# One-hot compares of a graph network kernel read their index row from PSUM instead of SBUF

## The chip, the cores and the metric

The kernel runs on one core of a Trainium2 chip. The metric is the device time of one execution in microseconds, as the median of several runs.

## The reference

Two graph layers over 6250 nodes and 100000 edges, sorted by destination. First three SAGE layers, each a mean over incoming edges and two products of 128 x 128:

```python
def _sage_layer(x, src, dst, Wl_i, bl_i, Wr_i):
    msg = x[src]
    agg = jax.ops.segment_sum(msg, dst, num_segments=N_NODES)
    cnt = jax.ops.segment_sum(jnp.ones((src.shape[0],), x.dtype), dst, num_segments=N_NODES)
    mean = agg / jnp.clip(cnt, 1.0)[:, None]
    return mean @ Wl_i + bl_i + x @ Wr_i
```

Then a gated graph convolution with 16 attributes for each edge (sigmoid times softplus of a linear map of both nodes and the attributes, summed by destination, batch norm, layer norm, relu), with a residual and a layer norm after either part.

## The kernel before, in words

**Tiles and windows.** The nodes are 49 windows of 128. The edges are cut into 832 tiles (`NS`) of at most 128 edges, and each tile belongs to one window. `dlo` holds, in column t, the row of the window to which each of the 128 edges of tile t goes; `srcs` holds the edges' source nodes; both stay in SBUF. `iota` is a tile of 128 x 128 in SBUF with 0 to 127 in each row.

**A SAGE layer** has two parts. The second, after the sums, makes the new features window by window (L999 to L1014 on VectorE, transposes and products on TensorE, copies on ScalarE) and writes the product to `y_dram`. The first sums the gathered rows and is a loop of 52 turns with 16 tiles each (`UB`), on four engines at once. For one tile:

- GpSimd (L421) gathers 128 rows of 512 bytes from `y_dram` to slot u of `msg` with an indirect DMA. Its indices come from `idx`.
- ScalarE (L677) copies eight columns of `srcs` to one half of `idx`, as soon as TensorE has summed the eight tiles that used that half's message slots one turn earlier (it waits for `tiles_summed`).
- VectorE makes the one-hot matrix of the tile (L963): `iota` is compared with one column of `dlo`, a scalar for each partition, and gives 128 x 128 fp32 in one of four slots of `oh4`.
- TensorE (L511) multiplies the one-hot matrix by the message slot into PSUM bank u mod 4. It waits for the gather, for the one-hot and for that bank's last add. An fp32 product shows as a pair of matmuls.
- VectorE (L974) adds the bank's 128 x 129 to the tile's window of `acc` (a dynamic offset); each add waits for the add before it.

VectorE's order in a turn is written out: load the 16 window offsets from `regs` (L946), one-hots 0, 1 and 2, add 0, one-hot 3, add 1, and so on, so that a one-hot stands two tiles ahead of its add. Before each of them stand register operations that compute the semaphore value to wait for or the offset (L971, L972, and those of L963 and L974); they run on VectorE's sequencer. Layer 3's turns 0 to 45 also split edge attributes in bf16 parts (L662, L667, L953) which SyncE writes back (L320).

**The convolution** (its one-hots and adds run from 4288 to 5672 us) gathers in the same manner (L439), four tiles a step. Its one-hots are made four tiles at a time by a tensor-tensor compare (L1156), its adds are L1127, its register operations L1125 among others.

**PSUM** is eight banks of 512 fp32. The sums use banks 0 to 3. `ps_tr` is banks 4 to 7 cut in 16 slots of 128; the transposes of the row numbers at the start use slots 0 to 6 and 8 to 14 (L500), those of the layers slots 0 to 6. The convolution uses all banks.

Of the kernel before, what the change touches and what calls it, by code (L numbers as in the profile page):

```python
# [5 lines left out]
P = 128  # L6
# [9 lines left out]
UB = 16  # L16
# [17 lines left out]
def build_gnn(nc, x, xT, src, dst, ea, eaT, w0, bl, blT, w1, we, b1, bn, out):  # L34
# [11 lines left out]
    with ctx:  # L46
        def sb(name, shape, dt=f32):
            return ctx.enter_context(nc.sbuf_tensor(name, shape, dt))
# [29 lines left out]
        dlo = sb("dlo", [P, NC * P])  # L78
# [4 lines left out]
        iota = sb("iota", [P, P])  # L83
        ident = sb("ident", [P, P])
# [26 lines left out]
        oh4 = work[:, 3584:4096].rearrange("p (u f) -> p u f", f=P)  # L111
# [72 lines left out]
        ps = ctx.enter_context(nc.psum_tensor("ps", [P, 8, 512], f32))  # L184
# [5 lines left out]
        ps_pre = ps[:, 0:4, :].rearrange("p (g b) (h f) -> p g (b h) f", g=2, h=2)  # L190
        ps_ohT = ps[:, 4:6, :].rearrange("p g (t f) -> p g t f", t=G)
        ps_agg = ps[:, 6:8, :].rearrange("p g (t f) -> p g t f", t=G)

        names = """const loads dnat w0_in xT_first xT_rest y_written products dve cnt S
            tki tab tab_back idx_given idx_sorted ea_sorted rows rowsf rows_tr dlo_ready srcs_ready
# [41 lines left out]
        def _(sp):  # L237
# [67 lines left out]
            for k, (_, part_) in enumerate(EA_GROUPS):  # L305
                sp.dma_start(we_rows[k * ED:(k + 1) * ED, :], we_part[:, part_, :]).then_inc(s["we_in"], 16)
# [8 lines left out]
            def store_parts(n):  # L315
                for part_, ready in enumerate(("ea_1", "ea_2", "ea_3")):
                    sp.wait_ge(s[ready], n + 1)
                    for k, (mine, _) in enumerate(EA_GROUPS):
                        if mine == part_:
                            sp.dma_start(parts_flat[k, :, bass.ds(n * EA_C, EA_C)], ea_part[part_])\  # L320
                                .then_inc(s["ea_written"], 16)
                sp.wait_ge(s["ea_written"], (n + 1) * (16 * len(EA_GROUPS)))
                sp.sem_inc(s["ea_free"], 1)
# [140 lines left out]
        def _(pe):  # L464
            te = nc.tensor
# [4 lines left out]
            for it in range(NCH):  # L470
# [3 lines left out]
                for b, wins in enumerate(PAIRS):  # L474
                    for u in wins:
                        w = it * CW + u
                        last = te.matmul(ps_prod[:, u, :], lhsT=xT_sb[:, w * P:(w + 1) * P], rhs=w0_sb[:, 0, :],
                                         start=True, stop=True)
# [16 lines left out]
                        .then_inc(s["f_rank"], 1)  # L495

            pe.wait_ge(s["rowsf"], 1)
            for c in range(2 * NC):
                rows, slot = (d_rowsf, c) if c < NC else (s_rowsf, c - NC + 8)
                last = te.transpose(ps_tr[:, slot, :], rows[:, c % NC * P:(c % NC + 1) * P], ident[:, :])  # L500
# [41 lines left out]
            with pe.Fori(0, NCH) as it:  # L542
# [6 lines left out]
                for b, wins in enumerate(PAIRS):  # L549
# [3 lines left out]
                    for h in range(2):  # L553
                        for u in wins:
                            last = te.matmul(ps[:, 2 + b % 2 if h else P_BANKS[b], u % 2 * 2 * F:(u % 2 + 1) * 2 * F],  # L555
                                             lhsT=hT[:, u, :],
                                             rhs=w1_sb[:, h * 2 * F:(h + 1) * 2 * F], start=True, stop=True)
# [58 lines left out]
            for w in range(0, NW, 4):  # L616
                n = min(4, NW - w)
                last = te.matmul(ps[:, 0, 0:n * F], lhsT=ones[:, :], rhs=a3[:, w:w + n, 0:F],
                                 start=w == 0, stop=w + n == NW)
            last.then_inc(s["bn_sum"], 1)  # L620
            for i, w in enumerate(range(0, NW, 4)):
# [3 lines left out]
                          rhs=work[:, 5376 + i % 2 * 512:5376 + i % 2 * 512 + n * F],  # L625
                          start=w == 0, stop=w + n == NW).then_inc(s["sq_used"], 1)
# [205 lines left out]
        def _(dve):  # L832
            v = nc.vector
# [111 lines left out]
            def load_windows(first):  # L945
                dve.reg_load(w_regs, regs[0:1, bass.ds(first, UB)])  # L946
                return [dve.snap(r, min_val=0, max_val=(NW - 1) * FA) for r in w_regs]  # L947

            def ea_rest(n, k):

                dve.wait_ge(s[f"ea_{k}"], n + 1)
                alone(dve)
                v.tensor_tensor(ea_chunk(n), ea_chunk(n), ea_part[k - 1], ALU.subtract).then_inc(s[f"ea_r{k}"], 1)  # L953

            def sage_adds(layer, a=0, b=NS // UB, split=False):
                with dve.Fori(a, b) as it:
                    wins = load_windows(it * UB)
                    first = layer * NS + it * UB

                    def onehot(u):  # L960

                        dve.wait_ge(s["tiles_summed"], first + u + 13)
                        v.tensor_scalar(oh4[:, u % 4, :], iota[:, :], dlo[:, bass.ds(it * UB + u, 1)], None,  # L963
                                        ALU.is_equal).then_inc(s["onehots"], 1)

                    onehot(0)
                    onehot(1)
                    for u in range(UB):
                        if u + 2 < UB:
                            onehot(u + 2)  # L970
                        dve.wait_ge(s["tiles_summed"], first + u + 17)  # L971
                        dve.wait_ge(s["tiles_added"], first + u + 4)  # L972
                        a = acc[:, bass.ds(wins[u], FA)]
                        v.tensor_tensor(a, a, ps[:, u % 4, 0:FA], ALU.add).then_inc(s["tiles_added"], 1)  # L974
                        if split and u % (UB // 2) == UB // 2 - 1:
                            ea_rest(it, u // (UB // 2) + 1)
# [288 lines left out]
```

## Time and profile before

| What | Value |
|---|---|
| Median of 3 runs | 5962.75 us (5954.95 to 5963.79) |
| Span of the profiled execution | 5833.6 us |
| TensorE matmul, busy | 2719.4 us (47%) |
| TensorE weight load, busy | 2017.8 us (35%) |
| VectorE, busy | 2564.2 us (44%) |
| ScalarE, busy | 1155.0 us (20%) |
| GpSimd, busy | 3317.1 us (57%) |

The span runs from the first to the last instruction of the program and is shorter than the time of a run, which holds the launch and the end as well. GpSimd's busy time in the sums is the issue of the indirect DMAs.

### The profile page before, as it was taken

What the parts mean: (1) busy time and instruction counts of PE and PEld (TensorE: products, weight loads), DVE (VectorE), ACT (ScalarE), POOL (GpSimd) and SP (SyncE); (2) the same over time, 40 slices, a digit from 0 to 9 for tenths busy, and PEclk for the clock granted to TensorE, in tenths of its full rate; (3) what the DMA queues carried; (4) which work ended last, traced back from release to release, by engine and by line L of the source; (5) the groups of instructions that cost most, each with busy time, mean ns of one, the idle gap of its engine ahead of it and who ended that gap; (6) DMA issues with size and microseconds to landing.
All of it is one profiled execution on the core that took longest, in us unless ns stands there. A gap on an engine that the chain in (4) does not pass through costs nothing. (4 is left out here: it accounts for less than half of the span.)

```text
span 5833.6 us, 67780 instructions
## 1 busy us (share of the span) xinstructions
PE 2719.4 (47%) x10689; PEld 2017.8 (35%) x10690; DVE 2564.2 (44%) x7859; ACT 1155.0 (20%) x2047; POOL 3317.1 (57%) x3391
## 2 busy tenths in 40 slices
PE   3334433345444334334433333333567666676761
PEld 2323322233222223333322223223445554554540
DVE  5333333334333333333433333333556666666667
ACT  1000000001000000000100000000256666666653
POOL 2566666663666665665455555555356566566644
PEclk6555555556555555555655555555688888888985
DMA  4111111111111111111222222222133333333320
GB/s 144 41 43 42 42 42 42 43 42 50 43 42 42 42 43 41 43 42 40 71 67 65 68 68 65 67 67 54 48 101 96 93 97 98 93 99 97 101 77 22
DMA packets 338000, 367.82 MB, mean 63 GB/s; under 512 B 183715, under 2 KB 268829, under 8 KB 337693
## 3 DMA queue, kind: packets, MB, share of 16 engines
q0 software_dynamic: 120256, 273.76, 17.6%
q1 hardware_dynamic: 215374, 89.93, 5.6%
q10 hardware_dynamic: 2352, 3.95, 0.2%
q14 instruction: 14, 0.11, 0.0%
q8 instruction: 4, 0.07, 0.0%
HBM read 322.39 MB, written 52.10 MB: 64 GB/s over the span
## 5 line engine op out<-in xcount | busy, mean ns | idle before, releaser
L421 POOL DMA_INDIRECT gath<-y_dram,idx x2496 | 2365.8, 948 | 1698.5 <-ACT idx L677 855.1
L511 PE MATMUL ps<-gath,work 128*128 128x129 f32 x4992 | 1556.4, 461 | 2416.6 <-issue 1255.4
L511 PEld LDWEIGHTS ps<-gath,work 128*128 128x128 f32 x4992 | 1166.5, 305 | 2806.9 <-issue 1507.7
L974 DVE TENSOR_TENSOR acc<-acc,ps 128x129 f32 x2496 | 723.4, 290 | 1800.3 <-issue 918.4
L439 POOL DMA_INDIRECT gath<-q_dram,idx x832 | 870.1, 1046 | 543.1 <-issue 273.8
L963 DVE TENSOR_SCALAR work<-iota,dlo 128x128 f32<-128x128 f32 x2496 | 724.0, 296 | 788.0 <-issue 691.3
L677 ACT COPY idx<-srcs 128x8 int32 (+1 forms) x312 | 61.6, 197 | 3507.4 <-PE ps L511 3124.7
L582 PE MATMUL ps<-pq,work 128*128 x1664 | 553.9, 435 | 147.4 <-issue 79.4
L582 PEld LDWEIGHTS ps<-pq,work 128*128 128x128 f32 x1664 | 289.6, 218 | 268.0 <-issue 207.9
L1127 DVE TENSOR_TENSOR acc<-acc,ps 128x128 f32 x832 | 233.7, 281 | 318.2 <-remote 231.1
L1137 DVE TENSOR_TENSOR work<-ps,gath 128x1024 f32<-128x1024 f32 x208 | 253.9, 1220 | 177.9 <-remote 87.7
L599 PE MATMUL ps<-work 128*128 128x128 f32 x1664 | 278.3, 319 | 38.0 <-DVE work L1164 27.2
L592 PE MATMUL ps<-ident,work 128*128 128x128 f32 x832 | 151.0, 310 | 266.4 <-DVE work L1156 171.2
L599 PEld LDWEIGHTS ps<-work 128*128 128x128 f32 x1664 | 238.1, 221 | 78.3 <-issue 70.2
L585 PE MATMUL ps<-we_rows,ea_sb 128*128 128x256 bf16 x832 | 245.0, 294 | 0.0
L766 ACT ACTIVATE work<-work 128x1024 f32<-128x1024 f32 x208 | 220.0, 1058 | 114.7 <-DVE work L1137 71.9
L774 ACT ACTIVATE work<-work 128x1024 f32<-128x1024 f32 x208 | 220.0, 1058 | 6.6
L592 PEld LDWEIGHTS ps<-ident,work 128*128 128x128 f32 x832 | 100.9, 155 | 338.1 <-DVE work L1156 203.7
L772 ACT ACTIVATE work<-work 128x1024 f32<-128x1024 f32 x208 | 216.4, 1040 | 0.0
L769 ACT ACTIVATE work<-work 128x512 f32<-128x512 f32 x208 | 130.3, 626 | 268.3 <-DVE work L1146 171.0
L780 ACT COPY work<-ps 128x512 f32<-128x512 f32 x208 | 121.4, 584 | 139.0 <-remote 84.5
L1156 DVE TENSOR_TENSOR work<-iota,dlo 128x512 f32<-128x512 f32 x208 | 141.8, 682 | 4.5 <-DMA q_dram<-work 4.5
(165 smaller groups left out, 1528.3 us busy)
## 6 DMA issues: line engine op xcount, KB each, us to landing
gath<-y_dram,idx POOLq DMA_INDIRECT x2496
ea_sb<-ea_parts SPq DMA_DIRECT2D x832, 32.0 KB
ea_parts<-pq SPq DMA_DIRECT2D x368, 68.0 KB
gath<-q_dram,idx POOLq DMA_INDIRECT x832
y_dram<-work SPq DMA_DIRECT2D x21, 448.0 KB
q_dram<-work SPq DMA_DIRECT2D x7, 896.0 KB, 4.1
eaT_sorted<-in_eaT SPq DMA_DIRECT2D x2, 3128.0 KB
pq<-eaT_sorted SPq DMA_DIRECT2D x46, 136.0 KB
```

Of the source, the lines that this page charges most:

```text
L421: pool.indirect_dma_start(msg[:, u, 0:F], None, y_dram, bass.IndirectOffsetOnAxis(ap=idx[:, u:u + 1], axis=0)).then_inc(s_msg[u], 16)
L439: pool.indirect_dma_start(qg[:, g, t, :], None, q_dram, bass.IndirectOffsetOnAxis(ap=idx[:, g * G + t:g * G + t + 1], axis=0))\
L511: te.matmul(ps[:, u % 4, 0:FA], lhsT=oh4[:, u % 4, :], rhs=msg[:, u, :], start=True, stop=True).then_inc(s["tiles_summed"], 1)
L582: te.matmul(o, lhsT=ohT[:, (slot - 1) % 2, t, :], rhs=pq[:, bass.ds(wins[(slot - shift) * G + t], 2 * F)], start=True, stop=False)
L585: last = te.matmul(o, lhsT=ea_sb[:, (slot - 1) % GB * G + t, :], rhs=we_rows[:, :], start=False, stop=True)
L592: last = te.transpose(ps_ohT[:, slot % 2, t, :], oh[:, slot, t, :], ident[:, :])
L599: last = te.matmul(ps_agg[:, (slot - 3) % 2, t, :], lhsT=oh[:, (slot - 3) % GB, t, :], rhs=mm[:, (slot - 3) % 2, t, :], start=True, stop=True)
L766: sc.activation(log_, pre[:, slot % 2, :, :], ACT.Abs).then_inc(s["absd"], 1)
L963: v.tensor_scalar(oh4[:, u % 4, :], iota[:, :], dlo[:, bass.ds(it * UB + u, 1)], None, ALU.is_equal).then_inc(s["onehots"], 1)
L974: v.tensor_tensor(a, a, ps[:, u % 4, 0:FA], ALU.add).then_inc(s["tiles_added"], 1)
L1127: v.tensor_tensor(a, a, ps_agg[:, slot % 2, t, :], ALU.add).then_inc(s["agg_added"], 1)
L1137: v.tensor_tensor(pre[:, slot % 2, :, :], ps_pre[:, slot % 2, :, :], qg[:, (slot - 2) % GB, :, :], ALU.add).then_inc(s["added"], 1)
```

## The change

The compare of the three SAGE layers reads its row 0..127 from PSUM. A matmul of the identity by `iota`, before the transposes of the row numbers, puts `iota` in the last quarter of bank 7, where it stays until the layers are done. The compare's output, its scalar operand, its waits and its place in VectorE's order stay as they are.

```diff
@@ -191,6 +191,8 @@
+        iota_ps = ps[:, 7, 3 * P:4 * P]
@@ -495,6 +497,8 @@
             pe.wait_ge(s["rowsf"], 1)
+
+            te.matmul(iota_ps, lhsT=ident[:, :], rhs=iota[:, :], start=True, stop=True)
             for c in range(2 * NC):
                 rows, slot = (d_rowsf, c) if c < NC else (s_rowsf, c - NC + 8)
                 last = te.transpose(ps_tr[:, slot, :], rows[:, c % NC * P:(c % NC + 1) * P], ident[:, :])
@@ -960,7 +964,7 @@
                     def onehot(u):
 
                         dve.wait_ge(s["tiles_summed"], first + u + 13)
-                        v.tensor_scalar(oh4[:, u % 4, :], iota[:, :], dlo[:, bass.ds(it * UB + u, 1)], None,
+                        v.tensor_scalar(oh4[:, u % 4, :], iota_ps, dlo[:, bass.ds(it * UB + u, 1)], None,
                                         ALU.is_equal).then_inc(s["onehots"], 1)
```

## Rows read from the trace of the kernel before

**Rows 1.** Instruction groups: line, engine, operation, tiles, count, busy us, mean ns, idle before, releasers.

```profile
L421 POOL DMA_INDIRECT gath<-y_dram,idx x2496 | 2365.8, 948 | 1698.5 <-ACT idx L677 855.1 <-issue 843.3
...
L963 DVE TENSOR_SCALAR work<-iota,dlo 128x128 f32<-128x128 f32 x2496 | 724.0, 296 | 788.0 <-issue 691.3 <-DVE acc L974 45.5 <-PE ps L511 31.3
```

**Rows 2.** Timeline of all engines, end of a layer-1 turn (start us, duration us, [idle before]).

```profile
618.48 0.28 DVE L963 TENSOR_SCALAR work<-iota,dlo 128x128 f32<-128x128 f32 x1
...
618.81 0.80 PE L511 MATMUL ps<-gath,work 128*128 128x129 f32 x2 [0.27 <-DVE work L963]
...
619.73 0.20 ACT L677 COPY idx<-srcs 128x8 int32 x1 [17.63 <-PE ps L511]
...
620.73 0.94 POOL L421 DMA_INDIRECT gath<-y_dram,idx  x1 [5.22 <-ACT idx L677]
```

**Rows 3.** Timeline of GpSimd, from that turn to the next.

```profile
621.97 0.95 POOL L421 DMA_INDIRECT gath<-y_dram,idx  x1 [0.30 <-issue]
...
625.73 0.98 POOL L421 DMA_INDIRECT gath<-y_dram,idx  x1 [0.30 <-issue]
...
635.76 0.95 POOL L421 DMA_INDIRECT gath<-y_dram,idx  x1 [0.30 <-issue]
637.01 0.95 POOL L421 DMA_INDIRECT gath<-y_dram,idx  x1 [0.30 <-issue]
...
645.70 0.94 POOL L421 DMA_INDIRECT gath<-y_dram,idx  x1 [5.24 <-ACT idx L677]
```

**Rows 4.** Windows of 5 us: busy us of PE, PEld, DVE, ACT, POOL; clock, DMA share, GB/s.

```profile
621.90:626.90 5.00, 4.61 (x18) 4.17 (x18) 3.97 (x17) 0.04 (x1) 3.82 (x4) 0.50 0.18 52
...
631.90:636.90 5.00, 1.60 (x4) 1.00 (x4) 0.80 (x3) 0.00 (x0) 3.78 (x4) 0.50 0.20 52
...
641.90:646.90 5.00, 1.60 (x4) 1.01 (x4) 1.48 (x6) 0.20 (x1) 0.94 (x1) 0.50 0.00 0
```

**Rows 5.** Timeline of VectorE where that turn slows down.

```profile
626.75 0.28 DVE L963 TENSOR_SCALAR work<-iota,dlo 128x128 f32<-128x128 f32 x1
628.99 0.29 DVE L974 TENSOR_TENSOR acc<-acc,ps 128x129 f32 x1 [1.96 <-issue]
629.20 0.28 DVE L963 TENSOR_SCALAR work<-iota,dlo 128x128 f32<-128x128 f32 x1
```

**Rows 6.** Instructions of one line, ns min/median/max: L971 at 621-627, 628-643 us; L963, layer 1.

```profile
L971 DVEq ALU_OP  x7: 21/40/40, 622.4 to 626.1; - x7
...
L971 DVEq ALU_OP  x5: 14/679/687, 628.2 to 640.9; - x5
...
L963 DVE TENSOR_SCALAR work<-iota,dlo x832: 273/285/530, 112.5 to 1408.3; 128x128 f32<-128x128 f32 x167
```

**Rows 7.** Groups on VectorE, shapes kept apart, columns as in rows 1.

```profile
L1127 DVE TENSOR_TENSOR acc<-acc,ps 128x128 f32 x832 | 233.7, 281 | 318.2 <-remote 231.1 <-PE ps L599 61.3 <-issue 24.0
...
L1156 DVE TENSOR_TENSOR work<-iota,dlo 128x512 f32<-128x512 f32 x208 | 141.8, 682 | 4.5 <-DMA q_dram<-work 4.5
...
L999 DVE SCALAR_TENSOR_TENSOR work<-acc,inv,pq 128x128 f32 x84 | 23.7, 351 | 5.8 <-PE ps L525 5.8
...
L1003 DVE COPY acc<-zero 128x903 f32 x12 | 7.6, 631 | 1.8
```

**Rows 8.** Timeline of VectorE between layers 1 and 2, two copies from PSUM.

```profile
1420.47 0.29 DVE L1013 COPY work<-ps 128x128 f32 x1 [1.01 <-PE ps L532]
1420.68 0.28 DVE L1014 COPY pq<-ps 128x128 f32 x1
```

**Rows 9.** Timeline of all engines in layer 3, end of a slow stretch.

```profile
3413.43 0.28 DVE L963 TENSOR_SCALAR work<-iota,dlo 128x128 f32<-128x128 f32 x1
...
3413.77 1.79 PE L511 MATMUL ps<-gath,work 128*128 128x129 f32 x6 [0.90 <-DVE work L963]
```

**Rows 10.** Register operations elsewhere: VectorE in the convolution (L1125), SyncE in layer 3 (L320).

```profile
L1125 DVEq ALU_OP  x612: 40/40/40, 4288.8 to 5656.5; - x153
...
L320 SPq MOVE ea_parts<-pq x321: 3/29/713, 2851.0 to 3899.9; - x161
```

## The prediction

> **What bounds the kernel now.** I read the grouped instructions first, then one turn of the gather loop in order of time, then stage windows inside that turn, and last the sequencer's rows of VectorE. The change touches only one group: L963, the one-hot compare, 2496 times, mean 296 ns, 724.0 us busy [rows 1]. That is 12% of the 5833.6 us span, so the first question is how much of it lies on the path. The three SAGE layers are 3 x 52 = 156 turns of 16 tiles, and the 2496 gathers of GpSimd (L421) show where the time goes: 2365.8 us busy, 1698.5 us idle before them, half of the idle time put down to the index copy on ScalarE [rows 1]. So GpSimd is the busiest engine in these layers but is not always running.
>
> In order of time the turn is plain. GpSimd starts a turn's first gather at 620.73 and the next turn's at 645.70 [rows 2, 3]: a turn is 24.97 us. In it 16 gathers follow each other every 1.25 us (0.95 us and 0.30 us between, [rows 3]), which is 20 us, and then comes an idle stretch of 5.22 us, released by the index copy [rows 2]. Going back along that chain: gather 620.73, index copy 619.73, last matmul 618.81, one-hot at 618.48, whose end at 618.76 is 50 ns before the matmul [rows 2]. So the last one-hot of each turn is on the path. The other fifteen need a look at why the last one is so late: the data of this turn had long been moved.
>
> The windows say that gathers move 52 GB/s evenly while GpSimd issues, and 0 GB/s in its pause [rows 4]. VectorE is not slow by its work: it is busy 3.97 of 5 us in one window of that turn and 0.80 of 5 us ten microseconds later [rows 4]. Its timeline shows a one-hot at 626.75 and the next add only at 628.99, after 1.96 us of idle time that nothing released ("issue") [rows 5]. The sequencer's rows give the cause in form, if not in origin: L971, one register operation before each add, has a median of 40 ns between 621 and 627 us and of 679 ns between 628 and 643 us, while the gathers run [rows 6]. At some 0.7 us for each sequencer instruction VectorE falls behind the gathers; when the transfers have stopped (0 GB/s from 641.9) [rows 4] it is quick again, and only after its last one-hots are the indices of the next gathers released. VectorE's sequencer during the gathers is what makes a turn 25 us and not 20. The one-hot's duration is not.
>
> **The change part by part.**
>
> *Price of one one-hot.* It has one tensor input, one output and a per-partition scalar. The tensor input moves to PSUM. The rows that give the price: an add of 128 elements with one input in PSUM takes 281 ns, two inputs in SBUF at 512 elements 682 ns [rows 7]. (682 - 281) / 384 = 1.044 ns an element, and 281 - 128 x 1.044 = 147 ns fixed: PSUM or SBUF makes no difference to the fixed part there. A copy of 903 elements from SBUF takes 631 ns [rows 7], (631 - 147) / 903 = 0.54 ns an element, two elements a cycle; a copy of 128 from PSUM takes 0.28 us [rows 8], one a cycle. A per-partition scalar costs 351 - 281 = 70 ns (L999 has one, L1127 none, both 128 elements) [rows 7]. So the one-hot of 285 ns (median) [rows 6] is 147 + 70 + 67, which is two elements a cycle; from PSUM it is one, 147 + 70 + 134 = 351 ns, **67 ns more**. Below, if it gains nothing from two a cycle now, 0; above, if it also loses the 80 ns by which the row pairs overlap today (add at 628.99, one-hot 0.21 us later, though the add takes 0.29) [rows 5], 150 ns. L1013 and L1014 both read PSUM and still start 0.21 us apart at 0.29 us each [rows 8], so I take 67.
>
> The Trainium skill has a rule that speaks against this change: "VectorE: DVE Perf Modes", section "Why PSUM operands drop a tier", says that the doubled rate in fp32 needs both SBUF read ports, and PSUM has one for this engine; the trace agrees (0.54 against 1.04 ns an element). The same page, in the section on the TRN2 errata, gives a fixed cost 62 cycles higher from PSUM than from SBUF, an estimate of 65 ns on top; by that the one-hot would be 416 ns and the sum below 14 + 7 + 0.8 - 1.7 - 3.6 = +16 us, 5979 us. The 281 ns of the add does not show it, and the measurement decides.
>
> *What of it is on the path.* In layers 1 and 2, of a turn's 16 one-hots the first ten run while VectorE is quick. What they delay is covered by the slow stretch behind them: there the sequencer delivers one instruction in 0.7 us whatever the engine does with the last, and the stretch ends when the transfers end. The next four lie in that stretch, one in 2 to 3 us, with over 1.5 us of idle time before most of the adds [rows 5]. The 16th is on the path. 104 turns x 0.067 = **+7.0 us**. In layer 3 the slow stretch lies elsewhere in the turn and the copy is released by a burst of matmuls (3413.77) behind the one-hot at 3413.43 [rows 9]; there too one one-hot sets the start of the burst and the others run beside the three tiles of that burst (1.79 us). 52 x 0.067 = **+3.5 us**, between 0 and twice that, since I looked at one turn of this form. If the cover of the slow stretch were gone, all ten would count (rival B).
>
> *The new matmul.* One more, fp32, on TensorE between the rounding of the row numbers and their transposes. The transposes wait behind it and the first gather's indices behind them, so it counts in full. A tile's matmul takes 0.80 us as a pair [rows 2]; **+0.8 us**, once. It writes the last quarter of bank 7, which the transposes (slots 0 to 14) and the sums (banks 0 to 3) leave alone, so no wait is added. No DMA, queue or semaphore changes.
>
> *What it gives back.* Mean minus median of the one-hots is 296 - 285 = 11 ns [rows 1, 6]: some wait for something now. On the path that is 156 x 0.011 = **-1.7 us**. In the quick stretch one gather in a turn takes 0.98 us where the others take 0.95 [rows 3]; if the one-hots cause it and stop doing so, -0.035 x 104 = **-3.6 us**.
>
> Sum: 7.0 + 3.5 + 0.8 - 1.7 - 3.6 = +6.0 us. The profiled execution spans 5833.6 us, to 5839.6; the median of the runs, 5962.75, lies 129 us above the span, for work outside it that nothing here changes. So 5962.75 + 6.0 = **5969 us**. About 0.2%, 12 us, is what a measurement of this kernel can tell from no change, and the forecast is inside it.
>
> **The rivals.**
>
> A, *faster, by the port.* The long register operations stand only where these one-hots stand: in the convolution, which has as many gathers a turn but no such compare, L1125 has 40 ns as minimum, median and maximum over 612 [rows 10]. If the compare's use of a second SBUF port against GpSimd's gathers causes them, moving the input to PSUM frees VectorE, and a turn falls to GpSimd's 20 us: 156 x 5.0 = -780 us, 5183 us. Against it: the sequencer of SyncE, which computes nothing, has the same 0.7 us operations in layer 3 (L320, 29 ns median, 713 ns maximum) [rows 10]; the stall is on register operations, 2 us after the last one-hot ended; and GpSimd's gathers stand as close where one-hots are dense (620.73 to 621.97) as where there is hardly one (635.76 to 637.01) [rows 2, 3]. The Trainium skill's page "SBUF — State Buffer", under "Who interferes with whom", says that such an operation and GpSimd's descriptor writing lock each other out for a whole instruction. By this rule the gathers should stretch when one-hots are dense; one a turn does, by 35 ns, and that is in the sum. 9%.
>
> A', *a small gain*: the two returns are real and the one-hot costs nothing more: 5962.75 + 0.8 - 1.7 - 3.6 = 5958; with the waits of all 16 one-hots of a turn on the path, 156 x 16 x 0.011 = 27 us less than 5963, 5933. Midway, 5945. 6% that it goes below -12 us.
>
> B, *slower, by a slow stretch of fixed length.* If the sequencer's slow stretch is a fixed number of instructions and not ended by the transfers, the ten quick one-hots count in full: 156 x 10 x 0.067 = +105 us, 6068 us. It decides where the last one-hot comes before the transfers are over; in the profile it comes over 1 us after, in a pause with 0 GB/s [rows 2, 4]. 6%.
>
> C, *slower, by the lost overlap*: 150 ns instead of 67 and two one-hots on the path in each turn: 156 x 0.15 x 2 = +47 us, 6009 us; with one, +23, 5986 us. It decides as soon as the one-hot behind an add starts 0.29 and not 0.21 us after it. 17%.
>
> D, *nothing happens*: the compare takes 285 ns from PSUM too, 5962 us. It is inside the forecast's band, with it 62%.
>
> **How the numbers follow.** Forecast and D 0.62, A 0.09, A' 0.06, B 0.06, C 0.17. Predicted time 5969. The range leaves A and B out, 0.15 together: from A' at 5945 to C at 6015. Faster by over 0.2%: A and A', 0.15. Slower by over 0.2%: B and C, 0.23. Within: 0.62.
>
> **What would show it.** L963 at 351 ns, all of them nearly equal (right), or at 285 (D) or above 400 (the skill's fixed cost). A turn from gather to gather of 25.04 us instead of 24.97. L971 with medians of 0.7 us still in the gathers' stretch; if they are gone, A holds. POOL's L421 mean at 945 instead of 948 ns. One-hot starts 0.21 us after an add's start, or 0.29 (C). What would make the prediction wrong: that the sequencer's slow stretch, whose origin the profile does not name, hangs on the compare after all, or that its length is set by something that I took for a fixed partner.

## The result and the profile after

| | before | after |
|---|---|---|
| Median | 5962.09 us (20 runs) | 5979.26 us (20 runs) |
| Lowest to highest | 5924.9 to 5972.14 us | 5951.72 to 6012.43 us |
| Ratio | | 1.0041, 95% interval 1.0026 to 1.0057 |
| Span of the profiled execution | 5833.6 us | 5970.0 us |

The kernel got slower by 0.3 to 0.6%: the medians differ by 17 us, the ratio gives 24 us, and its interval is 16 to 34 us. The profiled execution of after took 5971.78 us and spans 5970.0 us, so only 1.8 us lie outside the span. The 5833.6 us of before are therefore not the picture of a run of 5962 us: that execution was some 130 us shorter than the median of the 20 runs. The two first traces may not be subtracted from each other. What they show in kind holds: the same chain and the same stall.

The groups that answer [rows 1], from the page of after (L963 is L967 now, L421 is L423):

```profile
L423 POOL DMA_INDIRECT gath<-y_dram,idx x2496 | 2356.6, 944 | 1805.2 <-ACT idx L681 984.4 <-issue 820.8
...
L967 DVE TENSOR_SCALAR work<-ps,dlo 128x128 f32<-128x128 f32 x2496 | 847.4, 346 | 1020.4 <-issue 976.5 <-PE ps L515 20.4 <-DVE acc L978 17.0
```

The one-hot reads `ps` and takes 346 ns on average instead of 296. The single instruction has a narrow spread now, and the register operation before the add (L975, formerly L971, as in [rows 6]) still has its stalls:

```profile
L967 DVE TENSOR_SCALAR work<-ps,dlo x2496: 340/345/353, 112.3 to 4256.1; 128x128 f32<-128x128 f32 x192
...
L975 DVEq ALU_OP  x8: 27/40/1396, 608.7 to 613.9; - x8
...
L975 DVEq ALU_OP  x4: 689/700/1396, 613.9 to 625.9; - x4
```

Timeline of VectorE in that quick stretch and into the slow one, to be read beside [rows 5]:

```profile
611.78 0.29 DVE L978 TENSOR_TENSOR acc<-acc,ps 128x129 f32 x1
611.98 0.34 DVE L967 TENSOR_SCALAR work<-ps,dlo 128x128 f32<-128x128 f32 x1
...
612.91 0.29 DVE L978 TENSOR_TENSOR acc<-acc,ps 128x129 f32 x1
613.12 0.35 DVE L967 TENSOR_SCALAR work<-ps,dlo 128x128 f32<-128x128 f32 x1
615.35 0.29 DVE L978 TENSOR_TENSOR acc<-acc,ps 128x129 f32 x1 [1.89 <-issue]
```

A one-hot starts 0.20 us after its add, as before: the overlap of two readers of PSUM is kept. The end of the turn, all engines, to be read beside [rows 2]:

```profile
629.54 0.29 DVE L978 TENSOR_TENSOR acc<-acc,ps 128x129 f32 x1 [1.79 <-PE ps L515]
629.75 0.34 DVE L967 TENSOR_SCALAR work<-ps,dlo 128x128 f32<-128x128 f32 x1
630.04 0.29 DVE L978 TENSOR_TENSOR acc<-acc,ps 128x129 f32 x1
630.15 0.99 PEld L515 LDWEIGHTS ps<-gath,work 128*128 128x128 f32 x4 [1.84 <-DVE work L967]
630.15 1.29 PE L515 MATMUL ps<-gath,work 128*128 128x129 f32 x4 [1.54 <-DVE work L967]
630.24 0.34 DVE L967 TENSOR_SCALAR work<-ps,dlo 128x128 f32<-128x128 f32 x1
...
631.55 0.20 ACT L681 COPY idx<-srcs 128x8 int32 x1 [18.06 <-PE ps L515]
...
632.56 0.94 POOL L423 DMA_INDIRECT gath<-y_dram,idx  x1 [5.91 <-ACT idx L681]
```

The last burst holds two tiles' matmuls here (x4, 1.29 us), where the trace of before had one: the 15th one-hot (629.75) and the 16th (630.24) follow each other at once, because VectorE is one tile further behind. What releases the index copy is the same. It starts 0.97 us after the end of the 16th one-hot (630.58 to 631.55), as in before (618.76 to 619.73).

### The profile page after: what moved, and what is told of

Same layout as the page of the kernel before. It is cut to its first block and busy times, and to the rows that moved or that the text cites. A ratio compares the mean times of both kernels' runs of the same rounds, so it can differ in the third digit from the quotient of the medians.

```text
span 5970.0 us, 67784 instructions
## 1 busy us (share of the span) xinstructions
PE 2714.9 (45%) x10691; PEld 2037.0 (34%) x10692; DVE 2638.1 (44%) x7859; ACT 1153.7 (19%) x2047; POOL 3307.4 (55%) x3391
## 5 line engine op out<-in xcount | busy, mean ns | idle before, releaser
L423 POOL DMA_INDIRECT gath<-y_dram,idx x2496 | 2356.6, 944 | 1805.2 <-ACT idx L681 984.4
L515 PE MATMUL ps<-gath,work 128*128 128x129 f32 x4992 | 1539.1, 460 | 2536.3 <-DVE work L967 1322.9
L967 DVE TENSOR_SCALAR work<-ps,dlo 128x128 f32<-128x128 f32 x2496 | 847.4, 346 | 1020.4 <-issue 976.5
```

Source lines behind the costliest of these rows:

```text
L423: pool.indirect_dma_start(msg[:, u, 0:F], None, y_dram, bass.IndirectOffsetOnAxis(ap=idx[:, u:u + 1], axis=0)).then_inc(s_msg[u], 16)
L515: te.matmul(ps[:, u % 4, 0:FA], lhsT=oh4[:, u % 4, :], rhs=msg[:, u, :], start=True, stop=True).then_inc(s["tiles_summed"], 1)
L967: v.tensor_scalar(oh4[:, u % 4, :], iota_ps, dlo[:, bass.ds(it * UB + u, 1)], None, ALU.is_equal).then_inc(s["onehots"], 1)
```

## The experiments

The runs fell in two conditions, and that is the first finding. Each set of runs below shares one chip and its own runs of before. The four sets after the first comparison were on four different chips, so the record cannot tell the chip from the moment:

| Set | before | VectorE's sequencer |
|---|---|---|
| first comparison | 5962.09 us | stalls (0.70 us) |
| e1 to e4 | 4763.52 us | does not stall in any trace |
| e5, e7 | 5827.19 us | stalls |
| e9 to e11 | 4764.59 us | does not stall in any trace |
| e12 to e14 | 5941.77 us | stalls |

**Controls and the change where nothing stalls.** The kernel before, unchanged:

> The kernel before, unchanged, as a control: its trace comes from the same chip as those beside it. Ratio 1.000, not more than 0.2% off. In the first profiled execution of before the span was 5833.6 us though all its unprofiled runs were over 5924 us; every theory expects the span of this one near 5960 us, and a turn of the first two layers at 25.5 us and not at 24.97. If the turn is 25.5 us here, the difference of the two first traces (25.64 against 24.97) is mostly not the change's.

Measured: 4766.08 us, ratio 1.000 (0.9991 to 1.0009). It was not the turn of 25.5 us that I expected of every theory; a fifth of the time is gone. The rows of the control that answer [rows 6] and [rows 10], L971 and SyncE's L320, minimum, median and maximum in ns:

```profile
L971 DVEq ALU_OP  x2496: 40/40/40, 112.0 to 3331.5; - x192
...
L320 SPq MOVE ea_parts<-pq x352: 29/29/29, 2302.5 to 3174.0; - x176
```

2496 register operations, all of 40 ns, by the same program that has them at some 680 to 700 ns in the stalling stretches elsewhere. The groups of this trace:

```profile
L421 POOL DMA_INDIRECT gath<-y_dram,idx x2496 | 2359.2, 945 | 880.5 <-issue 854.0 <-ACT idx L677 26.5
...
L974 DVE TENSOR_TENSOR acc<-acc,ps 128x129 f32 x2496 | 725.0, 290 | 1557.9 <-PE ps L511 1543.1 <-issue 3.2 <-DVE acc L974 0.4
L963 DVE TENSOR_SCALAR work<-iota,dlo 128x128 f32<-128x128 f32 x2496 | 703.8, 289 | 292.5 <-issue 292.5
```

GpSimd waits 26.5 us for indices in all three layers (855.1 in [rows 1]), and VectorE waits for TensorE, which waits for gathers. The first layer's gathers run from 108.7 to 1153.1 us: 1044.4 us for 832, 1.255 us each. GpSimd sets the time.

The rest of the program, mostly the convolution, is longer under the stall too, though none of the edits touches it. From the end of layer 3's last gather to the end of the span it takes 1436.2 us in this trace and 1679.2 us in that of before, 243 us of the 1068 us between the two. There it is SyncE's sequencer that stalls, where it loads the edge attributes. The control, and then before:

```profile
L349 SPq MOVE ea_sb<-ea_parts x832: 29/29/38, 3428.9 to 4572.3; - x167
```

```profile
L349 SPq MOVE ea_sb<-ea_parts x832: 2/29/722, 4254.9 to 5641.0; - x167
```

How much it stalls varies from execution to execution: the same stretch takes 1718.1 us in after, and 1735.1, 1716.3 and 1753.0 us in e13, e14 and e12, which ran on one chip. A difference between the spans of two stalling traces holds that as well.

> The whole change. Theory L (only the last one-hot of a turn counts, 67 ns): +10 us, ratio 1.002. Theory M (two or three one-hots of the quick stretch at the end of a turn count, by their longer duration): +17 to +30 us, ratio 1.003 to 1.005, and the difference grows with the one-hot's duration. Theory S (a slower quick stretch costs sequencer instructions too, so more than the last ones count): over +40 us. Turn against the control's: L +0.07, M +0.13 to 0.2, S over +0.25 us.

Measured: 4763.69 us, 0.9997 (0.9988 to 1.0006), below all three theories, which reckon with the stall. The same comparison in another set:

> The kernel before again, for its trace beside the two that follow. Ratio 1.000 within 0.2%. If the sequencer stalls here (before at 5800 us or more), it gives the turn against which the change's is read; if not (near 4763 us), it only repeats the earlier control.

Measured: 4764.59 us, 0.9998 (0.9989 to 1.0007).

> The whole change, where the sequencer stalls. First comparison: ratio 1.0041. Theory L (the last one-hot alone, 60 ns): a turn 0.06 us longer than the control's, +10 us, 1.0017. Theory S (whatever is added in the quick stretch comes through in a small part, as the wide one-hots did with 75 of 437 us, 17%): 16 one-hots at 61 ns are 152 us over all turns, 17% of it +26 us, 1.0044, a turn 0.17 us longer, most of it in layer 3, where the wide ones showed 0.7 us a turn against 0.16 in the others. Where it doesn't stall: 1.000, as measured.

Measured: 4762.02 us, 0.9994 (0.9985 to 1.0003). Where the sequencer doesn't stall, 61 ns more on each one-hot cost nothing. Theories L and S are about the stalling condition, and this set says nothing on them.

**The compare without a per-partition scalar.**

```diff
-  v.tensor_scalar(oh4[:, u % 4, :], iota_ps, dlo[:, bass.ds(it * UB + u, 1)], None, ALU.is_equal)
+  v.tensor_tensor(oh4[:, u % 4, :], iota_ps, dlo[:, bass.ds(it * UB + u, 1)].to_broadcast([P, P]), ALU.is_equal)
```

> The change with the compare as a tensor-tensor compare: iota from PSUM, the column of dlo broadcast along the row, so that no per-partition scalar is read. One-hot 281 ns instead of 346 (change) and 285 (before). If the duration of the one-hot is the cause of the slowdown (L and M), the ratio to before is 1.000 within 0.1%. If reading PSUM as such costs (a PSUM access beside the matmuls' writes), it stays at 1.004. If the freed SBUF port is worth anything, this kernel is faster than before: by GpSimd's 0.035 us a turn, 4 us.

Measured where nothing stalls: 4764.32 us, 1.0001 (0.9992 to 1.001); its one-hot takes 286 ns. In the second such set:

> iota from PSUM by the tensor-tensor compare of 281 ns, where the sequencer stalls. Theories L and S put the slowdown on the one-hot's duration: ratio to before 1.000 within 0.1%, and a turn as long as the control's. If reading PSUM or the lost doubled rate costs in another way: 1.004 like the change. If freeing the port relieves the sequencer in part: below 1.000.

Measured: 4761.22 us, 0.9992 (0.9983 to 1.0001). The same compare with `iota[:, :]` from SBUF in the kernel before:

> The same tensor-tensor compare with iota from SBUF, so two SBUF inputs: 281 ns as well. Duration theory (L, M): same as the kernel with iota from PSUM, ratio 1.000 to before. Port theory: slower than the PSUM form, which leaves the second read port alone, by up to 10 us.

Measured: 4774.22 us, 1.0021 (1.0012 to 1.003), against 1.0001 for the PSUM form. Two inputs from SBUF do cost something, and it is on GpSimd. The first layer's gathers of this kernel, and of the change in e10, minimum, median and maximum in ns (the maximum of the two controls is 1015 in e1 and 1007 in e9):

```profile
L421 POOL DMA_INDIRECT gath<-y_dram,idx x832: 938/944/1065, 113.6 to 1156.2; - x167
```

```profile
L423 POOL DMA_INDIRECT gath<-y_dram,idx x832: 940/944/961, 107.5 to 1151.2; - x167
```

Reading from PSUM removes the long gathers (at most 961 ns), the two SBUF inputs lengthen some (1065 ns). The effect is there, and it is a few nanoseconds a gather on average. The compare itself takes 285 ns at the median from SBUF as from PSUM (e3).

**Work added to the quick stretch.** The change with the one-hots 0 to 6 of each turn at 512 columns instead of 128 (`iota` in the last 128):

```diff
-  v.tensor_scalar(oh4[:, u % 4, :], iota_ps, ...)
+  wide = u in range(0, 7)
+  v.tensor_scalar(oh4w[:, u % 4, :] if wide else oh4[:, u % 4, :], ps[:, 7, :] if wide else iota_ps, ...)
```

> The change, with the one-hots 0 to 6 of each turn four times as wide: they compare 512 columns of bank 7, of which the last 128 are the real ones and the rest go to unused columns, so that each takes 0.40 us more, 2.8 us a turn and 437 us in all 156 turns. Where VectorE's sequencer stalls (before near 5960 us, a turn of 25 us): by the theory that the quick stretch is covered by the slow one behind it, under +20 us; by the theory that it counts in full (rival B of the prediction), +437 us. Where it doesn't stall (before near 4763 us, a turn of 20 us that GpSimd's 16 gathers of 1.25 us fill): +0 us, since VectorE then waits over 1 us a tile for the next gather.

Measured where it stalls: 5902.22 against 5827.19 us, 1.0124 (1.0097 to 1.0152), +75 us for 437 us of added work and the change itself: far from rival B's 437, but above the 20 that the other theory allowed. The layers' lengths tell where. First and last gather of layer 1 and of layer 3 here:

```profile
L424 POOL DMA_INDIRECT gath<-y_dram,idx x832: 942/947/962, 114.1 to 1416.4; - x167
...
L424 POOL DMA_INDIRECT gath<-y_dram,idx x832: 942/947/3022, 2815.8 to 4213.6; - x167
```

and of before (the first profile, of 5833.6 us; it is not of this set, whose runs of before are 5808 to 5834 us, but near them):

```profile
L421 POOL DMA_INDIRECT gath<-y_dram,idx x832: 939/945/1004, 108.8 to 1404.1; - x167
...
L421 POOL DMA_INDIRECT gath<-y_dram,idx x832: 939/945/3029, 2799.4 to 4153.4; - x167
```

Layer 1: 1302.3 against 1295.3 us, +7 us for 52 x 2.8 = 146 us of added work. The slow stretch does cover the quick one there. Layer 3: 1397.8 against 1354.0 us, +44 us, the change's own part included. There it covers only some two thirds: in most turns of layer 3 GpSimd's pause stands before the turn's first gather and not before its ninth, the copy that ends it waits for the eighth tile, and so the wide one-hots 0 to 6 lie in or shortly before the burst that releases it.

**Work added to the last one-hot of each half.**

```diff
-  wide = u in range(0, 7)
+  wide = u in (7, 15)
```

> The change, with only the one-hots 7 and 15 of each turn four times as wide, 0.40 us more each. Where the sequencer stalls: theory L (the last one-hot, whose matmul releases the index copy and so the next gathers, counts in full and the rest do not) expects +62 us against the change, near 1.014 to before; theory S (every one-hot counts at about 17%) expects 2 x 0.40 x 156 x 0.17 = +21 us, near 1.008. Where it doesn't stall: 1.000.

Measured where it stalls: 6032.68 us, 1.0161 (1.0136 to 1.0187). Beside it the change, in the same set:

> The whole change. Where the sequencer stalls: 1.0017 by theory L, 1.0044 by theory S, 1.0041 in the first comparison. Where it doesn't stall: 1.000.

Measured: 5977.48 us, 1.0069 (1.0046 to 1.0091). The wide ones cost 55 us on top of the change, near the 62 of theory L and far from the 21 of theory S. One turn's end of the change, and then of the wide kernel:

```profile
627.31 0.35 DVE L967 TENSOR_SCALAR work<-ps,dlo 128x128 f32<-128x128 f32 x1 [0.42 <-remote]
...
627.80 0.34 DVE L967 TENSOR_SCALAR work<-ps,dlo 128x128 f32<-128x128 f32 x1
...
629.11 0.20 ACT L681 COPY idx<-srcs 128x8 int32 x1 [18.02 <-PE ps L515]
```

```profile
637.32 0.34 DVE L969 TENSOR_SCALAR work<-ps,dlo 128x128 f32<-128x128 f32 x1
...
637.81 0.74 DVE L969 TENSOR_SCALAR work<-ps,dlo 128x512 f32<-128x512 f32 x1
...
639.52 0.20 ACT L682 COPY idx<-srcs 128x8 int32 x1 [18.01 <-PE ps L516]
```

From the start of the 15th one-hot to the index copy 1.80 us, and 2.20 us with 0.40 us more in the 16th: in full. From the end of the 16th it is 0.97 us in both. The three layers are longer by 14.8, 20.9 and 19.9 us than in e13's trace (first gather to end of the last), where one wide one-hot a turn makes 20.8.

**The same duration as before, from PSUM.** The tensor-tensor compare again, beside e12 and e13:

> iota from PSUM by the tensor-tensor compare of 281 ns. Where the sequencer stalls: 1.000 if the one-hot's duration is the cause, 1.004 like the change if reading PSUM is, below 1.000 if freeing the port relieves the sequencer. Where it doesn't stall: 1.000.

Measured: 5963.63 us, 1.0039 (1.0018 to 1.0059), 14 us below the change. The end of a turn:

```profile
617.68 0.29 DVE L967 TENSOR_TENSOR work<-ps,dlo 128x128 f32<-128x128 f32 x1 [0.41 <-remote]
...
618.17 0.28 DVE L967 TENSOR_TENSOR work<-ps,dlo 128x128 f32<-128x128 f32 x1
...
619.42 0.20 ACT L681 COPY idx<-srcs 128x8 int32 x1 [18.09 <-PE ps L515]
```

1.74 us from the 15th one-hot to the index copy where the change has 1.80: the 60 ns of duration, once a turn. Both start the 16th 0.49 us after the 15th, so the 15th's longer duration costs nothing, and from the 16th's end it is 0.97 us again. The lengths of layer 3, first and last gather, of the change (e13) and of this one:

```profile
L423 POOL DMA_INDIRECT gath<-y_dram,idx x832: 941/947/3025, 2849.8 to 4240.4; - x167
```

```profile
L423 POOL DMA_INDIRECT gath<-y_dram,idx x832: 941/947/3026, 2833.9 to 4212.1; - x167
```

Layer 3: 1390.6 against 1378.2 us, 12.4 us for 60 ns; layer 1 in the same traces 1324.2 against 1318.4, 5.8 us. These traces must be read with care: e14's profiled execution was the fastest of its 12 (5931.14 us against a median of 5963.63), and 24 of the 47 us between the two spans lie outside the gathers of the three layers, where the code is the same. What repeats is layer 3's turn. Over 37 turns in the middle of the layer it has a mean of 27.05 us in after, 27.02 in e13, 27.42 in e12 (the 0.40 us of its wide eighth one-hot, in full) and 26.81 in e14. In layer 1 the same mean is 25.62 in after, 25.53 in e13 and 25.42 in e14, so two traces of the change differ there nearly as much as the two kernels do. One turn's last part in layer 3, from the fifth one-hot to the copy, in e13 and then in e14:

```profile
3492.91 0.35 DVE L967 TENSOR_SCALAR work<-ps,dlo 128x128 f32<-128x128 f32 x1
...
3495.86 0.20 ACT L681 COPY idx<-srcs 128x8 int32 x1 [17.28 <-PE ps L515]
```

```profile
3498.66 0.28 DVE L967 TENSOR_TENSOR work<-ps,dlo 128x128 f32<-128x128 f32 x1
...
3501.49 0.20 ACT L681 COPY idx<-srcs 128x8 int32 x1 [18.11 <-PE ps L515]
```

2.95 against 2.83 us: 0.12 of the 0.21 us by which the turns differ. The rest lies before that burst.

That the ratio did not fall to 1.000 is a miss for both theories: 22 us (10 to 35 by the interval) of the change's 36 in this set are not the one-hot's duration.

**Fewer instructions.** One compare of 128 x 512 for four tiles, with eight one-hot slots, in the kernel before:

```diff
-  v.tensor_scalar(oh4[:, u % 4, :], iota[:, :], dlo[:, bass.ds(it * UB + u, 1)], None, ALU.is_equal)
+  v.tensor_tensor(oh8[:, g % 2 * G:(g % 2 + 1) * G, :], iota[:, :].unsqueeze(1).to_broadcast([P, G, P]),
+                  dlo[:, bass.ds(it * UB + g * G, G)].unsqueeze(2).to_broadcast([P, G, P]), ALU.is_equal)
```

> The kernel before with one tensor-tensor compare for four tiles (128 x 512, 682 ns) in place of four compares, eight one-hot slots and one wait on them for four tiles: 12 compares and some 24 to 36 register operations fewer in each turn of about 106 VectorE instructions. Where the sequencer stalls: by the theory that the turn is set by the number of sequencer instructions at 0.7 us each, -2 to -5 us a turn, 300 to 780 us in all, down to GpSimd's 20 us a turn; by the theory that the stalls come with each compare (the port), also faster, but the register operations L971 that are left keep 0.7 us or lose it alike. Where it doesn't stall: 0, or up to +10 us for the two SBUF inputs, as the tensor-tensor compare from SBUF had it.

Measured where it stalls: 5594.82 us against 5827.19, 0.9598 (0.9573 to 0.9623). The kernel that beats both, by 4%, though by 232 us and not the 300 to 780 expected. Its gathers got longer, 971 ns on average against 948 in before, beside a compare of two SBUF inputs and 512 columns. The stalls are not gone with 12 of 16 compares (L973 is L971 of before; layer 2):

```profile
L973 DVEq ALU_OP  x821: 1/40/1395, 1400.1 to 2622.9; - x165
```

The edit also loosens TensorE's waits (one for four tiles) and takes fewer compares' time from VectorE, so the 4% are not shown to come from the number of instructions alone. It wasn't tried where nothing stalls; GpSimd sets the time there.

## Why the prediction was right or wrong

The range (5945 to 6015) held 5979.26. The case with the highest chance, within 0.2%, did not come: the interval lies wholly above it, and 17 to 24 us stand against 6 predicted. The sign and the size came out near what I had given rival C, but not by its mechanism. That the range held is in part luck: its upper end came from rival C (which gives 6009 and not 6015), whose mechanism did not occur.

**Price of one one-hot: right.** 67 ns predicted, 345 - 285 = 60 ns measured at the median. The parts hold within 10 ns: without the scalar the compare takes 285 ns at one element a cycle, from PSUM (e3) as from SBUF (e4), where 281 was reckoned, and the scalar adds 60 and not 70. The trace contradicts the Trainium skill's fixed cost of a PSUM source ("VectorE: DVE Perf Modes", the section on the TRN2 errata), by which it would have been 416 ns by the prediction's estimate. It agrees with the same page of the Trainium skill in its section "Why PSUM operands drop a tier". That the sum by that fixed cost, 5979 us, is the time that was measured is chance, since the one-hot takes 345 ns. The lost overlap (C) did not occur: 0.20 us from add to one-hot.

**One one-hot on the path in layers 1 and 2: right in place, and in size at the release.** It is the 16th: in before, after, e12, e13 and e14 the copy starts 0.97 us after its end, so 0.06 us more in it is 0.06 us a turn, 104 x 0.06 = 6.2 us against 7.0 predicted. The sum had counted ten, four and one one-hots and left out the 15th; it costs nothing, since the next add starts 0.28 us after it whether it takes 0.29 or 0.35. The layers' lengths say less: e13 against e14 gives 5.8 us in layer 1 and 5.0 in layer 2, and two traces of the change differ by as much (layer 1 takes 1330.9 us in after and 1325.2 in e13). The gather at 620.73, which I had called a turn's first, is its ninth: in layers 1 and 2 GpSimd's pause stands there in most turns. Rival B, that the quick stretch counts in full, fell with e5: 7 of 146 us in layer 1, and 75 of 437 in all.

**Layer 3: the term that was mis-sized.** +3.5 us predicted, up to 7. For 60 ns it measured 12.4 us, 0.21 to 0.24 us a turn. I had looked at one turn and taken the one-hots within its burst to be hidden beside TensorE. Some are not: from the fifth to the copy the burst is 0.12 us longer, twice the 60 ns, as would follow if each add and one-hot of VectorE waits for those in front of it. Where the other 0.1 us a turn arises, before the burst, is not shown. e5 shows the same from the other side, 44 us in layer 3 against 7 in layer 1. Terms for the duration then sum to 6.2 + 12.4 = 19 us, against 10.5; between the medians of e13 and e14 it is 14.

**What it gives back: nothing to be seen.** L423's mean of 944 ns seemed to be the predicted return, but e13, with the same code, has 947, and before where nothing stalls has 945. What did go are the longest gathers, 1004 to 962 ns in layer 1. By e10 against e9 at most 7 us in 4764, and the interval holds zero.

**Rival A: wrong.** The stall stayed with the SAGE compare off the second port (700 ns in after). Its premise, that the long operations stand only where these one-hots stand, did not hold in the trace of before either: SyncE's L349 in the convolution has operations of 722 ns. The kernel alone doesn't make the stall, since the same program has none of it in two sets.

**What I had wrong beneath all of this.** I read "129 us outside the span" where there are 2, and so took one execution of 5833.6 us to be the picture of runs of 5962. And I wrote the stall into the kernel as if it were its own. Where it is absent the change costs nothing that is seen (0.9997 and 0.9994, both intervals within 0.15% of 1); the effect was seen only where the sequencer stalls.

**What stays open.** In e14 a part of 22 us (10 to 35) is not explained by the one-hot's duration, nor by the added matmul (0.8 us once). Its one-hot is as long as that of before, it reads PSUM, and TensorE's program has one instruction more. No run separates these, and no profile of before was taken in that set. Two things as large as the rest are not the change: the untouched rest of the program differs by up to 37 us between this set's traces, and the runs of before rise in the order in which they are listed, from a mean of 5932 us in the first eight to 5954 in the last eight. In the first comparison (17 to 24 us) the duration alone could carry nearly all of it; the intervals of the two sets, 16 to 34 us and 27 to 54 us, overlap. The origin of the stall is open as well: that it appears only while gathers run or within 4 us of one, on VectorE and SyncE, is shown; why in some sets and not in others is not.

## What to carry to other kernels

Moving its operand to PSUM took this fp32 tensor-scalar compare from two elements a cycle to one, 60 ns for 128 columns, and what it freed on GpSimd's side was worth less than 0.2% even in a loop that GpSimd bounds. Price an edit against the burst that releases the next stage, counting each instruction in it, and look at several turns of each layer, since the same loop can be bound at another place in another layer. Where a sequencer's own operations are long, try fewer instructions first: merging four compares brought 4% where 60 ns on each moved 0.2%, though that run changed waits as well.

## What the runs showed of the hardware that I had not expected

- The same program takes 4764 or 5827 to 5962 us in different sets of runs, 22 to 25% more. In the traces it goes with register operations of VectorE and SyncE that take 0.70 us instead of 29 to 40 ns while indirect gathers run; those of ScalarE and GpSimd take at most 0.18 us in any trace. One of 33 runs of before in the set at 4763.52 us took 5348 us, so the condition may come for part of an execution too; no profile shows it.
- A profiled execution can be 2% shorter than the runs beside it (5833.6 us against a median of 5962.09 and at least 5924.9), so a span should be checked against the runs before a sum is built on it.
- Four times the width on seven one-hots a turn, 146 us of added VectorE work, moved layer 1 by 7 us (e5 against the first profile of before).
